# Order of the filter tables and a one-piece accumulating store in a depthwise layer on one core

## The chip, the cores and the metric

The kernel runs on one core of one Trainium2 chip. The metric is the time of one execution in microseconds (us) on the device. The kernel before was run three times: 5993.56, 6000.67 and 6012.33 us, median 6000.67. A further execution was profiled, and all rows below come from it.

## What is computed

The input x is 8 images of 32 channels of 512 x 512 float32. Two layers follow each other, each of the form x + f(normalised x), where the normalisation takes mean and variance over groups of two channels.

```python
x = x + _L0_conv_ref(_gn(x), L0_conv_weight, L0_conv_bias)
x = x + _L1_conv_ref(_gn(x), L1_conv_conv_w, L1_conv_conv_b)
```

Layer one is a quantised 3 x 3 convolution. Layer two first mixes the channels (a 1 x 1 convolution, `feat`), pools `feat` to a 5 x 5 filter for each image and channel, and applies each filter to its own channel (depthwise, 5 x 5, same size):

```python
feat = jnp.einsum('bihw,oi->bohw', x, conv_w) + conv_b[None, :, None, None]
filt = jnp.einsum('kh,bchw,lw->bckl', Ph, feat, Pw)
out = jax.lax.conv_general_dilated(inp, w, window_strides=(1, 1), padding=p,
        dimension_numbers=('NCHW', 'OIHW', 'NCHW'), feature_group_count=B * C)
```

The change touches only the second part of layer two, the depthwise product and its store.

## The kernel before

The kernel is one program of stages: `weights_and_masks`, `quantised_conv` (layer one, whose result x1 it writes to the output tensor in HBM), `statistics_of_x1`, `filters` (which writes the filters as tables to a scratch tensor in HBM), and `depthwise`, which this text is about.

`depthwise` walks through the 8 images, each cut into `BLOCKS` = 9 blocks of `ROWS_OUT` = 57 output rows (the last has 56), and each block into `STEPS` = 8 steps of four output channels. One step is a tile; an image has 72. Two kinds of product are made on TensorE in the same step. The pointwise product (lines 1053 to 1055) makes `feat` for the next block; the banded product (`banded`, line 1074, 36 matmuls a step) applies the filters to the block before, with a band matrix made from a table as the weights. Rows of the image lie in partitions, so that a tile of the result is 57 partitions of 4 channels x 512 columns.

The engines work in this order in one step. ScalarE splits x1 into a high part (`high`, line 966) and DVE into a low part (`low`, line 998); both copy the pointwise product out of PSUM (lines 979 and 1024); both evict half of the banded product into the slot `xr` of the tile (lines 988 and 1031). GpSimd then adds the slot to the output in HBM by an accumulating DMA (line 925), whose rows of 512 columns are single pieces of 2 KB.

There are `XR_SLOTS` = 4 slots. Before the eviction of tile m both engines wait in `wait_slot` until the store of tile m - 4 has landed (semaphore `stored[m % 4]`). The store is made as two transfers, of 48 rows (`SPLIT`) and of the other 9 (or 8 in the last block); each raises the semaphore by 16, so a slot counts 32 a tile. PSUM has two buffers for the banded product, which TensorE can refill only after both evictions.

SyncE issues all loads from one in-order queue. `load_x1` (line 851) loads a block of x1 for the block after the next, as four transfers. It waits until DVE has split the block whose buffer it takes, which is near step 6. `load_table` (lines 871 and 872) loads a quarter of the filter tables, eight channels, as four transfers of 48 or 13 rows and a bias transfer. There is one table buffer `tt` of 32 channels, so a quarter for the next image may be loaded only when the last block's steps have used it: quarter g is free after step 2g + 1. TensorE waits for quarter g (`t_loaded[g]`) at step 2g of the new image's first block. `group` on SyncE sets the order at the change of images (`j == N`): the quarters 0 and 1 stand at s = 5 and 7, x1 at s = 6, and quarters 2 and 3 follow at s = 7. Since every one of these places has its own wait, the number s only fixes the order: quarter 0, x1, quarter 1, 2, 3.

Of the kernel before, what the change touches and what calls it, by code (L numbers as in the profile page):

```python
# [5 lines left out]
ALU = mybir.AluOpType  # L6
# [33 lines left out]
STEPS = 8  # L40
XR_SLOTS = 4
# [3 lines left out]
SPLIT = 48  # L45
# [138 lines left out]
START = 1  # L184
# [572 lines left out]
def depthwise(nc, nb, k, rstd, table_d, bias_d, out):  # L757
# [6 lines left out]
    with ExitStack() as ctx:  # L764
# [17 lines left out]
        stored = [ctx.enter_context(nc.semaphore(f"c_stored{i}")) for i in range(XR_SLOTS)]  # L782
# [5 lines left out]
        band_done, even_out, odd_out = sem("c_band_done"), sem("c_even_out"), sem("c_odd_out")  # L788
        N = BLOCKS
        TILES = N * STEPS  # L790
# [3 lines left out]
        def valid(i):  # L794

            return (2 if i == 0 else 0), min(ROWS_IN, H + 2 - ROWS_OUT * i)

        def rows_out(i):
            return min(ROWS_OUT, H - ROWS_OUT * i)

        def xr_rows(m, lo, hi):

            base = PR * (m % XR_SLOTS % 2)
            return xr[base + lo:base + hi, m % XR_SLOTS // 2, :, :]
# [8 lines left out]
        def count(p, e, each, n):  # L813

            return p * (2 * each) + (e * each + n)

        def own(j):
            return j // N, j % N

        def another(p, e):  # L820

            return not (isinstance(p, int) and p == PAIRS - 1 and e == 1)

        def run(eng, group):

            group(0, 0, 0, True, False)
            if PAIRS > 1:
                with eng.Fori(0, PAIRS - 1) as p:
                    for e in range(2):
                        for j in range(1, N + 1):  # L830
                            group(p, e, j, True, True)
            for e in range(2):
                for j in range(1, N + 1):
                    group(PAIRS - 1, e, j, e == 0 or j < N, True)

        def x_slot(e, j):
            return (e * N + j) % 2

        def loads_of(p, e, j):

            return p * (N * Q * 16) + ((e * N + j) // 2 + 1) * (Q * 16)

        def load_x1(eng, p, e, j):

            if (e, j) not in ((0, 0), (0, 1)):
                eng.wait_ge(zl_done, count(p, e, STEPS * N, STEPS * (j - 1)) + START)
            de, i = own(j)
            lo, hi = valid(i)
            r0 = ROWS_OUT * i - 2
            for q in range(Q):  # L850
                eng.dma_start(xt[C * q:C * q + C, x_slot(e, j), lo:hi, :],  # L851
                              x1v[e + de::2][p, q, :, r0 + lo:r0 + hi, :]).then_inc(x1_loaded[x_slot(e, j)], 16)
# [3 lines left out]
        @block.sync  # L856
        def _(sp):

            def load_last_edge(p, e):

                sp.dma_start(tt[EDGE:EDGE + 1, :, :, :, :].rearrange("k o t w m -> k o (t w m)"),
                             bias_d[2:3, e::2, :, :][:, p, :, :]).then_inc(edge_loaded, 16)

            def load_table(p, e, g):
                for a in range(2):
                    for lo, hi in ((0, SPLIT), (SPLIT, ROWS_IN)):

                        src = table_d[e:nb:2][p, a, 8 * g * TROW + lo:8 * (g + 1) * TROW]
                        src = bass.AP(tensor=src.tensor, offset=src.offset, ap=[[1, hi - lo], [1, 8 * TROW]])
                        dst = tt[ROWS_IN * a + lo:ROWS_IN * a + hi, 8 * g:8 * g + 8, :, :, :]  # L870
                        sp.dma_start(dst.rearrange("k o t w m -> k (o t w m)"), src).then_inc(t_loaded[g], 16)  # L871
                sp.dma_start(tt[MAIN:EDGE + 1, 8 * g:8 * g + 8, :, :, :].rearrange("k o t w m -> k o (t w m)"),
                             bias_d[0:2, e::2, :, :][:, p, 8 * g:8 * g + 8, :]).then_inc(t_loaded[g], 16)

            def group(p, e, j, pointwise, banded):
                if not banded:
                    load_x1(sp, p, e, 0)
                    load_x1(sp, p, e, 1)
                    for g in range(4):
                        load_table(p, e, g)  # L880
                for s in range(STEPS):

                    if pointwise and j == N and s in (5, 7):
                        sp.wait_ge(band_done, count(p, e, TILES, TILES - STEPS + s - 3) + START)
                        load_table(p, e + 1, (s - 5) // 2)
                    if pointwise and j == N and s == 7:
                        for g in (2, 3):
                            sp.wait_ge(band_done, count(p, e, TILES, TILES - STEPS + 2 * g + 2) + START)
                            load_table(p, e + 1, g)
                    if s == 6 and pointwise and (j + 2 < N or another(p, e)):  # L890
                        load_x1(sp, p, e, j + 2)
                    if banded and j == 3 and s == 2:

                        sp.wait_ge(band_done, count(p, e, TILES, STEPS) + START)
                        load_last_edge(p, e)

            sem.start(sp)
            sp.wait_ge(cleared, 1 + START)
            run(sp, group)

        @block.gpsimd
        def _(pool):
            for m in range(XR_SLOTS):
                pool.dma_start(starter[0:1, m:m + 1], rstd[0:1, 0:1]).then_inc(stored[m], 16)  # L904

            for slot in range(2):
                pool.memset(feat[96:P, slot, 0, :, :], 1.0).then_inc(started, 1)  # L907
            pool.wait_ge(started, 6 + START)
            pool.memset(feat[:, :, :, :, 0:1].rearrange("p a b c d -> p (a b c) d"), 0.0)
            pool.memset(feat[:, :, :, :, FP - 1:FP].rearrange("p a b c d -> p (a b c) d"), 0.0).then_inc(cleared, 1)  # L910
            pool.wait_ge(cleared, 1 + START)

            def group(p, e, j, pointwise, banded):
                if not banded:
                    return
                if pointwise:

                    pool.wait_ge(x1_loaded[x_slot(e, j)], loads_of(p, e, j) + START)
                for s in range(STEPS):
                    m = STEPS * (j - 1) + s  # L920
                    n, r0 = rows_out(j - 1), ROWS_OUT * (j - 1)
                    pool.wait_ge(odd_out, count(p, e, TILES, m + 1) + START)
                    pool.wait_ge(even_out, count(p, e, TILES, m + 1) + START)
                    for lo, hi in ((0, SPLIT), (SPLIT, n)):
                        pool.dma_start(out[e::2][p, 4 * s:4 * s + 4, r0 + lo:r0 + hi, :].rearrange("c h w -> h c w"),  # L925
                                       xr_rows(m, lo, hi), accum_op=ALU.add).then_inc(stored[m % XR_SLOTS], 16)

            run(pool, group)
            for m in range(XR_SLOTS):
                pool.wait_ge(stored[m], nb * (TILES // XR_SLOTS) * 32 + 16)  # L930

        def positions(e, j, part):

# [18 lines left out]
                    tps[PR * h:PR * h + n, m % 2, :, :])  # L952

        def wait_slot(eng, p, e, m):
            eng.wait_ge(stored[m % XR_SLOTS], count(p, e, TILES // XR_SLOTS * 32, m // XR_SLOTS * 32) + 16)

        @block.scalar
        def _(act):
# [193 lines left out]
```

## Time and profile before

| | before |
|---|---|
| median of 3 runs | 6000.67 us (5993.56 to 6012.33) |
| profiled execution, its own time | 5992.25 us |
| its span | 5990.5 us |
| TensorE busy | 4829.2 us, 81% of the span |
| VectorE (DVE) busy | 4582.7 us, 76% |
| ScalarE (ACT) busy | 3994.4 us, 67% |
| GpSimd (POOL) busy | 1384.6 us, 23% |
| mean granted TensorE clock | 0.909 of full speed |
| layer two (first to last banded product) | 2722.8 to 5978.4 us of the span |

A row of a profile says what an engine did or what it waited for. PE is TensorE, PEld its weight load, DVE is VectorE, ACT is ScalarE, POOL is GpSimd, SP is SyncE; SPq is SyncE's queue, on which DMAs are issued. L1074 is line 1074 of the kernel. All times are us unless marked. An arrow `<-` between an engine's line and something else means "was released by". "DMA share" is the mean busy share of the core's 16 DMA engines; it can be above 1 since packets overlap. "Landing" is the time from a DMA's issue to its completion.

### The profile page before, as it was taken

What the parts mean: (1) busy time and instruction counts of PE and PEld (TensorE: products, weight loads), DVE (VectorE), ACT (ScalarE), POOL (GpSimd) and SP (SyncE); (2) the same over time, 40 slices, a digit from 0 to 9 for tenths busy, and PEclk for the clock granted to TensorE, in tenths of its full rate; (3) what the DMA queues carried; (4) which work ended last, traced back from release to release, by engine and by line L of the source; (5) the groups of instructions that cost most, each with busy time, mean ns of one, the idle gap of its engine ahead of it and who ended that gap; (6) DMA issues with size and microseconds to landing.
All of it is one profiled execution on the core that took longest, in us unless ns stands there. A gap on an engine that the chain in (4) does not pass through costs nothing.

```text
span 5990.5 us, 113135 instructions
## 1 busy us (share of the span) xinstructions
PE 4829.2 (81%) x43798; PEld 3263.0 (54%) x43798; DVE 4582.7 (76%) x5363; ACT 3994.4 (67%) x2509; POOL 1384.6 (23%) x1698
## 2 busy tenths in 40 slices
PE   0767767666667767918998989989989899899899
PEld 0111111111111111207988979979979789799798
DVE  6787878777787878747887868868868778688686
ACT  1646565655555556807877868868868778688686
POOL 0111111111111111112332323323323333233233
PEclk9888878888888888958999999989999999999999
DMA  9999999999999998949999999999999999999997
GB/s 263 278 276 301 301 287 302 281 302 273 319 261 322 271 312 242 287 96 184 180 196 179 180 193 183 181 190 182 188 192 180 197 179 180 188 189 178 188 190 125
DMA packets 1065164, 1347.06 MB, mean 225 GB/s; under 512 B 78330, under 2 KB 636666, under 8 KB 1060602
## 3 DMA queue, kind: packets, MB, share of 16 engines
q1 hardware_dynamic: 749506, 657.45, 49.3%
q0 software_dynamic: 240000, 537.11, 39.9%
q10 hardware_dynamic: 75072, 144.72, 8.3%
q8 instruction: 364, 5.96, 0.4%
q14 instruction: 222, 1.82, 0.1%
HBM read 800.10 MB, written 538.84 MB: 224 GB/s over the span
## 4 chain that ended last, share of the span: by engine, by line
PE 48%; SPq 4%; DMA 2%; DVE 0%; issue 0%; POOL 0%; ACT 0%; DVEq 0%; POOLq 0%; ACTq 0%
PE c_tps L1074 36%; PE c_cps L1053 4%; PE c_cps L1054 4%; PE c_cps L1055 4%; SPq L851 3%; DMA c_tt<-bias_scratch 2%; SPq L871 1%; DMA c_x<-out_dram 1%; DVE c_z L998 0%; POOL c_feat L907 0%; ACT c_z L966 0%; DVE c_xr L1031 0%; POOL c_starter L904 0%; POOL out_dram L925 0%; ACT c_feat L979 0%
## 5 line engine op out<-in xcount | busy, mean ns | idle before, releaser
L1074 PE MATMUL c_tps<-c_feat,c_tt 123*128 123x256 f16 (+1 forms) x20736 | 2385.6, 273 | 169.3 <-DMA c_tt<-bias_scratch 167.5
L1074 PEld LDWEIGHTS c_tps<-c_feat,c_tt 123*128 123x128 f16 (+1 forms) x20736 | 1998.8, 98 | 428.1 <-DMA c_tt<-bias_scratch 134.8
L925 POOL DMA_DIRECT2D out_dram<-c_xr x1152 | 1056.5, 1054 | 2266.3 <-DVE c_xr L1031 2105.9
L440 PE MATMUL b_ps<-b_xq,w0main 128*128 128x512 bf16 x3072 | 950.1, 415 | 679.5 <-ACT b_q L398 540.3
L966 ACT ACTIVATE c_z<-c_x,c_rs 128x976 f16<-128x976 f32 x576 | 1150.2, 1997 | 116.1 <-DMA c_x<-out_dram 116.1
L1031 DVE TENSOR_SCALAR c_xr<-c_tps 57x1024 f32<-57x1024 f32 (+1 forms) x576 | 701.5, 1218 | 686.1 <-PE c_tps L1074 686.1
L998 DVE SCALAR_TENSOR_TENSOR c_z<-c_x,c_rs,c_z 128x976 f16<-128x976 f32 x576 | 1105.9, 1920 | 69.6 <-ACT c_z L966 47.0
L398 ACT ACTIVATE b_q<-b_ps,q_bias 128x1024 int8<-128x1024 f32 x512 | 547.6, 1115 | 787.3 <-DVE b_x L518 728.8
L988 ACT ACTIVATE c_xr<-c_tps 57x1024 f32<-57x1024 f32 (+1 forms) x576 | 639.2, 1110 | 629.0 <-PE c_tps L1074 628.9
L440 PEld LDWEIGHTS b_ps<-b_xq,w0main 128*128 128x128 bf16 x3072 | 225.6, 101 | 1351.3 <-issue 1094.1
L453 PE MATMUL b_ps<-b_xq,w0edge 64*32 64x512 bf16 x3048 | 918.5, 411 | 0.0
L450 PE MATMUL b_ps<-b_xq,w0edge 64*32 64x512 bf16 x3048 | 915.7, 411 | 0.0
L1053 PE MATMUL c_cps<-w_high,c_z 128*128 128x128 f16 x4608 | 813.4, 221 | 124.4 <-DVE c_z L998 112.9
L979 ACT ACTIVATE c_feat<-c_cps 122x1024 f16<-122x1024 f32 x576 | 822.7, 1428 | 121.3 <-PE c_cps L1055 119.3
L573 POOL DMA_DIRECT2D out_dram<-b_x x512 | 298.9, 584 | 2254.8 <-DVE b_cols L533 2061.7
L1024 DVE TENSOR_TENSOR c_feat<-c_cps,c_feat 122x1024 f16<-122x1024 f32 x576 | 810.2, 1407 | 7.9 <-ACT c_feat L979 7.7
L1055 PE MATMUL c_cps<-w_high,c_z 128*128 128x128 f16 x4608 | 811.7, 220 | 0.0
L1054 PE MATMUL c_cps<-w_low,c_z 128*128 128x128 f16 x4608 | 811.2, 220 | 0.0
L477 DVE BATCH_NORM_STATS2 b_stats_x<-b_stream 128x6 f32<-128x512 f32 x672 | 414.4, 680 | 438.8 <-DMA b_stream<-in_x_dram 401.9
L529 DVE BATCH_NORM_STATS2 b_stats<-b_x 128x6 f32<-128x408 f32 (+5 forms) x1520 | 645.3, 500 | 3.9
L518 DVE SCALAR_TENSOR_TENSOR b_x<-b_q,b_x 128x2048 f32<-128x2048 int8 x256 | 574.8, 2281 | 65.4 <-ACT b_q L398 65.4
L383 ACT ACTIVATE b_x<-b_x,b_shift,b_scale 128x4096 int8<-128x4096 f32 x128 | 487.0, 3805 | 139.8 <-issue 101.8
(131 smaller groups left out, 2732.2 us busy)
## 6 DMA issues: line engine op xcount, KB each, us to landing
out_dram<-b_x POOLq DMA_DIRECT2D x512, 512.0 KB, 11.2
out_dram<-c_xr POOLq DMA_DIRECT2D x576, 384.0 KB, 7.9
c_x<-out_dram SPq DMA_DIRECT2D x224, 976.0 KB, 21.9
b_stream<-in_x_dram SPq DMA_DIRECT2D x672, 256.0 KB, 12.7
b_x<-in_x_dram ACTq DMA_DIRECT2D x276, 512.0 KB, 13.3
b_x<-in_x_dram SPq DMA_DIRECT2D x276, 512.0 KB, 12.4
c_tt<-table_scratch SPq DMA_DIRECT2D x64, 576.0 KB
out_dram<-c_xr POOLq DMA_DIRECT2D x512, 72.0 KB, 9.2
```

What stands on the lines that cost most here:

```text
L440: return pe.matmul(ps[:, g % 3, j, :], k.w0main[:, d, :, :].rearrange("p r o -> p (r o)"), xq[:, n % XQ_SLOTS, 2 * i + j, d:d + W], start= ...
L450: pe.matmul(ps[0:C, g % 3, j, :], k.w0edge[P // 2:P, d, :], xq[P // 2:P, (m - 1) // JB % XQ_SLOTS, (m - 1) % JB, d:d + W], start=False, st ...
L453: pe.matmul(ps[P - C:P, g % 3, j, :], k.w0edge[0:P // 2, d, :], xq[0:P // 2, (m + 1) // JB % XQ_SLOTS, (m + 1) % JB, d:d + W], start=False ...
L925: pool.dma_start(out[e::2][p, 4 * s:4 * s + 4, r0 + lo:r0 + hi, :].rearrange("c h w -> h c w"), xr_rows(m, lo, hi), accum_op=ALU.add).then ...
L966: act.activation(split_part(0, part), positions(e, j, part), ACT.Identity, scale=scale_of(e, j)).then_inc(zh_done, 1)
L979: act.activation(dst, cps[0:MAIN, s % 2, :, :].rearrange("p j (q o) -> p o q j", q=Q), ACT.Identity).then_inc(fh_done, 1)
L998: dve.scalar_tensor_tensor(split_part(1, part), positions(e, j, part), scale_of(e, j), split_part(0, part), ALU.mult, ALU.subtract).then_i ...
L1024: dve.tensor_tensor(lo, cps[0:MAIN, s % 2, :, :].rearrange("p j (q o) -> p o q j", q=Q), hi, ALU.subtract).then_inc(fl_done, 1)
L1053: pe.matmul(dst, zh, wh, start=True, stop=False)
L1054: pe.matmul(dst, zh, wl, start=False, stop=False)
L1055: last = pe.matmul(dst, zl, wh, start=False, stop=True)
L1074: last = pe.matmul(tps[:, s % 2, o % 4, :], tt[0:rows, o, tp, 2 * d:2 * d + 2, :].rearrange("k w m -> k (w m)"), feat[0:rows, (e * N + i) ...
```

## The change

On SyncE, at the change of images, quarter 1 of the table is issued ahead of the load of x1: the order becomes quarter 0, quarter 1, x1, quarter 2, quarter 3. Each quarter's wait is for the same step as before. On GpSimd the two accumulating transfers of a tile become one of all its rows (57, or 56 in the last block), and the counts of the slot semaphores are halved accordingly.

```diff
                 for s in range(STEPS):

-                    if pointwise and j == N and s in (5, 7):
-                        sp.wait_ge(band_done, count(p, e, TILES, TILES - STEPS + s - 3) + START)
-                        load_table(p, e + 1, (s - 5) // 2)
-                    if pointwise and j == N and s == 7:
+                    if pointwise and j == N and s in (2, 4):
+                        sp.wait_ge(band_done, count(p, e, TILES, TILES - STEPS + s) + START)
+                        load_table(p, e + 1, s // 2 - 1)
+                    if s == 6 and pointwise and (j + 2 < N or another(p, e)):
+                        load_x1(sp, p, e, j + 2)
+                    if pointwise and j == N and s == STEPS - 1:
                         for g in (2, 3):
                             sp.wait_ge(band_done, count(p, e, TILES, TILES - STEPS + 2 * g + 2) + START)
                             load_table(p, e + 1, g)
-                    if s == 6 and pointwise and (j + 2 < N or another(p, e)):
-                        load_x1(sp, p, e, j + 2)
...
-                    for lo, hi in ((0, SPLIT), (SPLIT, n)):
-                        pool.dma_start(out[e::2][p, 4 * s:4 * s + 4, r0 + lo:r0 + hi, :].rearrange("c h w -> h c w"),
-                                       xr_rows(m, lo, hi), accum_op=ALU.add).then_inc(stored[m % XR_SLOTS], 16)
+                    pool.dma_start(out[e::2][p, 4 * s:4 * s + 4, r0:r0 + n, :].rearrange("c h w -> h c w"),
+                                   xr_rows(m, 0, n), accum_op=ALU.add).then_inc(stored[m % XR_SLOTS], 16)
...
-                pool.wait_ge(stored[m], nb * (TILES // XR_SLOTS) * 32 + 16)
+                pool.wait_ge(stored[m], nb * (TILES // XR_SLOTS) * 16 + 16)
...
-            eng.wait_ge(stored[m % XR_SLOTS], count(p, e, TILES // XR_SLOTS * 32, m // XR_SLOTS * 32) + 16)
+            eng.wait_ge(stored[m % XR_SLOTS], count(p, e, TILES // XR_SLOTS * 16, m // XR_SLOTS * 16) + 16)
```

## Rows read from the trace of the kernel before

**Rows 1.** The page's chain that ended last: shares of the span by line.

```profile
PE c_tps L1074 36%; PE c_cps L1053 4%; PE c_cps L1054 4%; PE c_cps L1055 4%; SPq L851 3%; DMA c_tt<-bias_scratch 2%; SPq L871 1%; DMA c_x<-out_dram 1%; DVE c_z L998 0%; POOL c_feat L907 0%; ACT c_z L966 0%; DVE c_xr L1031 0%; POOL c_starter
```

**Rows 2.** The chain in time at the first image change: start, us, what.

```profile
3096.88 3.95 PE c_tps L1074 x36
...
3148.34 13.50 DMA c_tt<-bias_scratch
3161.89 5.72 PE c_tps L1074 x36
...
3168.95 3.95 PE c_tps L1074 x36
...
3174.24 3.95 PE c_tps L1074 x36
```

**Rows 3.** TensorE's waits (total us, times, longest): layer two, then 3100 to 3200 us.

```profile
PE c_tps L1074 <- DMA c_tt<-bias_scratch: 167.5, 7, 29.1
...
PE c_tps L1074 <- DMA c_tt<-bias_scratch: 27.7, 1, 27.7
```

**Rows 4.** SyncE's timeline at the first image change: start, us, line, transfers.

```profile
3095.44 8.66 SPq L871 DMA_DIRECT2D c_tt<-table_scratch  x4
3104.29 0.24 SPq L872 DMA_DIRECT2D c_tt<-bias_scratch  x1
3114.84 23.97 SPq L851 DMA_DIRECT2D c_x<-out_dram  x4
3139.09 9.07 SPq L871 DMA_DIRECT2D c_tt<-table_scratch  x4
3148.34 0.24 SPq L872 DMA_DIRECT2D c_tt<-bias_scratch  x1
```

**Rows 5.** Stretches: length, busy PE, PEld, DVE, ACT, POOL; PEclk, DMA share, GB/s.

```profile
3115.00:3135.00 20.00, 19.07 (x220) 17.21 (x217) 16.33 (x12) 16.20 (x12) 5.91 (x8) 1.00 1.13 211
3135.00:3162.00 27.00, 0.11 (x1) 0.12 (x2) 2.39 (x2) 2.37 (x2) 1.74 (x2) 0.55 1.10 209
```

**Rows 6.** DMA issues, whole span: count, KB each, median us to landing.

```profile
out_dram<-c_xr POOLq DMA_DIRECT2D x576, 384.0 KB, 7.9
c_x<-out_dram SPq DMA_DIRECT2D x224, 976.0 KB, 21.9
...
c_tt<-table_scratch SPq DMA_DIRECT2D x64, 576.0 KB
out_dram<-c_xr POOLq DMA_DIRECT2D x512, 72.0 KB, 9.2
...
c_tt<-table_scratch SPq DMA_DIRECT2D x64, 156.0 KB
...
c_tt<-bias_scratch SPq DMA_DIRECT2D x32, 24.0 KB
...
c_starter<-rstd POOLq DMA_DIRECT2D x4, 0.0 KB, 2.5
```

**Rows 7.** GpSimd's timeline after the stall: start, us, [idle before].

```profile
3169.68 1.87 POOL L925 DMA_DIRECT2D out_dram<-c_xr  x2 [32.94 <-DVE c_xr L1031]
3174.97 1.83 POOL L925 DMA_DIRECT2D out_dram<-c_xr  x2 [3.42 <-DVE c_xr L1031]
```

**Rows 8.** DMA traffic 5933.2 to 5939.2 us, one tile's store and no loads.

```profile
DMA packets 289, 0.48 MB, mean 81 GB/s; under 512 B 60, under 2 KB 60, under 8 KB 288
...
q0 software_dynamic: 288, 0.47, 57.2%
...
out_dram<-c_xr POOLq DMA_DIRECT2D x2, 384.0 KB, 4.8
out_dram<-c_xr POOLq DMA_DIRECT2D x2, 72.0 KB, 5.0
```

**Rows 9.** The store queue 3134 to 3142 us, beside x1's loads: packets, MB, share.

```profile
q0 software_dynamic: 490, 0.79, 55.2%
```

**Rows 10.** GB/s of all DMA in 40 slices, 3200 to 3242 us.

```profile
GB/s 241 218 214 232 279 197 181 209 198 262 244 225 220 272 178 178 196 195 200 189 216 139 74 77 82 174 149 39 78 183 145 132 163 151 193 215 212 252 217 209
```

## Prediction

> **What bounds the kernel now.** I read the chain that ended last first: it runs mostly on TensorE, in the banded product of line 1074 [rows 1]. In layer two a step is 5.29 us, the distance of two banded starts [rows 2], and there are 8 images x 9 blocks x 8 steps = 576 of them, 3,047 us. The list of waits comes second: line 1074 waits for only one thing, the table loads, 7 times for 167.5 us together and 29.1 us at most [rows 3]. Seven is the number of image changes. The third view, SyncE's timeline around the first change, shows why: table 0 is issued at 3095.44, then four loads of x1 from 3114.84 to 3138.8, and only then table 1, whose last piece is issued at 3148.34 and lands 13.50 us later, at 3161.84 [rows 2, 4]. In that instant line 1074 starts again [rows 2]; without the wait its start would have been 27.7 us earlier, at 3134.2 [rows 3]. Last, the table of stretches says what table 1 waited for: while TensorE stood still the DMA share was 1.10 and 209 GB/s moved, and just before it 1.13 [rows 5]. The sixteen DMA engines had no air at all; the table was late because they were full, not only because it was issued late.
>
> **Part one, the order of the tables.** SyncE's order at an image change was table 0, x1, table 1, 2, 3; it becomes table 0, 1, x1, 2, 3. Each table is still four pieces and a bias, (576 + 156) x 2 + 24 = 1,488 KB [rows 6]; nothing is added. Table 1's channels are free after the last block's step 3, at 3096.88 + 3.95 = 3100.83 [rows 2], so it can follow table 0, whose issue ends at 3104.53 [rows 4]. Its data would pass before x1's and be there by 3134.2: step 2 of the new image no longer waits. What is late next is table 2, which step 4 needs, two steps later at 3134.2 + 2 x 5.29 = 3144.7, and which still stands behind x1 (3.9 MB). The DMA engines must move the same bytes as before up to table 1's landing, plus table 2 (1.52 MB) and the stores of the two tiles that TensorE now makes meanwhile (2 x 0.47 MB): 2.46 MB at 209 GB/s are 11.8 us. Table 2 so lands at 3161.84 + 11.8 = 3173.6, and step 4 started at 3174.24 before [rows 2]. Gain: 0.6 us a change, 4 us in seven. The stall moves from step 2 to step 4 and is 3173.6 - 3144.7 = 28.9 us there in place of 27.7; the two steps that stood behind it, 12.4 us with their slow start [rows 2], stand ahead of it and take 10.6. The moved issue has x1 behind it: four loads come up to 1.52 MB / 209 GB/s = 7.3 us later, about 3168, and they are read first some steps after step 4, so nobody waits. The bounds: at best the queue had room, table 2 lands when table 1 did, and two steps are saved each time, 7 x 10.6 = 74 us; at worst table 1 itself is some 2 us late, 15 us. I take 4 us, since the share of over 1.0 leaves no room [rows 5].
>
> **Part two, one store of 57 rows.** It removes one issue on GpSimd per tile. GpSimd spends 1.8 us of each step on both and idles 3.4 us before the next [rows 7]; nobody waits for it but the landing, so this is worth nothing. What counts is when the transfer lands: tile m+4 may be evicted only when tile m's store is in. A store is issued 3169.68 - (3161.89 + 5.72) = 2.1 us after its last product [rows 2, 7], and the slot is wanted four steps later, so the budget is 4 x 5.29 - 2.1 = 19.1 us. Now the two pieces take 7.9 and 9.2 us [rows 6], 4.8 and 5.0 us where no load runs beside them [rows 8].
>
> How 57 rows are shared among 16 engines no row shows directly. What the last-image window shows: one tile puts 288 packets on the queue, 60 of them tiny [rows 8]. 57 rows x 4 channels are 228 pieces of 2 KB, which leaves 60 = 2 x 16 semaphore updates + 28, and 28 is 7 x 4: seven engines got fillers in place of the 9-row piece's four entries. So whole rows go to engines, one each on nine. 48 is three each on sixteen. Every transfer of this queue has equal shares (32, 48, 9, 8 rows). 57 = 3 x 19 has equal shares only on three engines (or one): 19 rows, 76 pieces each. Uneven shares would be four rows on most of fifteen engines, 16 pieces. I take three engines, as the nearest rows all have equal shares.
>
> The price of a piece: a transfer of nothing lands in 2.5 us [rows 6], so alone it is (4.8 - 2.5) / 12 = 0.19 us; with x1's loads in flight the queue moved 0.79 MB, 386 pieces, in 8 us on 16 engines, 0.33 us a piece [rows 9]. 76 pieces then land in 2.5 + 76 x 0.19 = 17 us alone, and in 2.5 + 76 x 0.33 = 28 us beside loads. The first is under the budget, the second over it. Loads fill about 29 us of a block of 42.3: in the 42 us window the first 21 slices and the last 7 of 40 are the fast ones [rows 10]. A transfer of over 20 us seldom lies wholly inside, so I take the middle, 23 us: a slot turns round in 23 + 2.1 us, a step in 25.1 / 4 = 6.3. 29 us hold 4.6 such steps, the other 3.4 take 18 us, the block 47 in place of 42.3: 4.7 us x 64 blocks = 300 us. (The ninth block of each image has 56 rows, equal on fourteen engines, 16 pieces: no cost.) Bounds: 17 us throughout costs nothing; 28 us throughout makes every step (28 + 2.1) / 4 = 7.5 us, x 512 steps = +1,140 us. Less than nothing only if fewer semaphore updates relieve the engines: 16 of 288 packets, tiny ones, under 5 us in all.
>
> The Trainium skill, page DMA: Bandwidth & Descriptors, section on why a DMA increments its semaphore by 16, says that a copy runs on the largest number of engines up to 16 that divides its slowest dimension; by it 57 rows have 3 and 56 have 14, as I take them. The same page's rules for kernel authors speak the other way for the merge, since two transfers to disjoint partitions share the engines anyway; by them this part would cost nothing.
>
> **Sum.** The profiled execution is 5992.25 us (span 5990.5), 8 us under the median of the three runs shown. 5992 - 4 + 300 = 6288, say 6290.
>
> **The rivals.** (a) Uneven shares: 57 rows on fifteen engines. 16 pieces land in 2.5 + 16 x 0.33 = 7.8 us, far inside 19.1; the time is 5988, no change. For it: the fillers show that the hardware can pad an engine that has nothing to do [rows 8]. Against it: no transfer here is uneven. The same page of the Trainium skill names an exception in which some copies from GpSimd use all 16 engines with rounded-up shares; no run here shows it, and it would be this case. (b) Three engines, but GpSimd's queue gets a larger part of each engine than 0.33 us a piece says: 76 pieces land within 19 us (0.22 us each), and again nothing changes, about 5990. For it: a single queue's 0.19. (c) The other side: the table's stall was one of order. Place: the image change; price: the two steps, 74 us, so 5918, provided that (a) or (b) holds too. It decides where table 2 lands before 3171, that is, where x1 isn't delayed by table 1; the engines would need 2.5 us of air between 3104 and 3134. Against it the share of 1.13 [rows 5]. Half of its price would already be seen. (d) The load's rate on three shared engines falls below what I take and the transfers run at 28 us or more: 5992 + 1,140 = 7,130.
>
> **How the numbers follow.** Three engines with a price (forecast, with (d) at its upper end): 0.68. (a) 0.15 and (b) 0.07: no change. (c) 0.10. A measurement of this kernel can tell about 0.3% (18 us) from none. So faster 0.10, same 0.22, slower 0.68. The forecast case's own range is 6080 to 6800. The whole range must take in (a) and (b) and leaves out (c)'s full price and (d)'s extreme: 5960 to 6800.
>
> **What would show it.** Right: GpSimd's store, now 456 KB, lands in about 17 us in the last block but one and over 20 us beside loads, 8 us at the 56-row blocks; DVE's and ScalarE's evictions of lines 1031 and 988 wait for the DMA of c_xr, and line 1074 for them; steps of over 6 us in the first two thirds of a block. Line 1074's waits for tables stay near 24 us a change, two steps later than before, with the bias of table 2 last. Wrong: landings of 8 to 10 us and steps of 5.29 (then (a)); or the waits for tables down to about 14 us each (then (c)).

## The result, and the profile after

The changed kernel takes 6335.86 us (6317.32 to 6360.93, 4 runs) against 6000.73 us of the kernel before, a ratio of 1.0558 with a 95% interval of 1.0523 to 1.0593. The forecast was 6290 us, the range 5960 to 6800. The profiled execution has a span of 6348.3 us, 357.8 us more than before.

The page of the changed kernel, in the parts that answer to [rows 1, 6]: the DMA queue of the stores, the chain that ended last, the two lines of TensorE and GpSimd, and the stores with their landing. All line numbers of `depthwise` behind the store are one lower than before.

```profile
q0 software_dynamic: 722304, 541.01, 41.8%
...
DMA out_dram<-c_xr 23%; SPq L851 9%; PE c_tps L1073 8%; DMA c_x<-out_dram 6%; DVE c_z L997 2%; DMA c_tt<-bias_scratch 2%; SPq L871 1%; DVE c_xr L1030 1%; PE c_cps L1052 1%; PE c_cps L1054 1%; PE c_cps L1053 1%; ACT c_xr L987 0%; ACT c_z L965 0%; POOL c_feat L907 0%; ACT c_feat L978 0%
...
L1073 PE MATMUL c_tps<-c_feat,c_tt 123*128 123x256 f16 (+1 forms) x20736 | 2415.1, 275 | 244.5 <-DMA c_tt<-bias_scratch 230.0
...
L924 POOL DMA_DIRECT2D out_dram<-c_xr x576 | 1098.0, 1906 | 2579.3 <-DVE c_xr L1030 2102.7
...
out_dram<-c_xr POOLq DMA_DIRECT2D x512, 456.0 KB, 19.8
c_x<-out_dram SPq DMA_DIRECT2D x224, 976.0 KB, 26.4
```

The chain that ended last no longer runs on TensorE's line (8% in place of 36%) but on the landing of the stores, 23%, and on x1's loads, 9% for their issue and 6% for their landing. A store lands in 19.8 us in place of 7.9 and 9.2 [rows 6]. And one issue on GpSimd costs 1906 ns, 1098.0 us in all, where the 1,152 issues of before took 1056.5 us of busy time together; the merge has saved GpSimd nothing.

The waits in layer two of the changed kernel (total us, times, longest):

```profile
DVE c_xr L1030 <- DMA out_dram<-c_xr: 497.5, 201, 11.3
ACT c_xr L987 <- DMA out_dram<-c_xr: 470.8, 191, 11.2
...
PE c_tps L1073 <- DMA c_tt<-bias_scratch: 230.0, 8, 40.2
PE c_cps L1052 <- DVE c_z L997: 227.4, 124, 21.4
...
ACT c_z L965 <- DMA c_x<-out_dram: 171.6, 38, 25.3
```

The same list of the kernel before has these two rows for the last two:

```profile
PE c_cps L1053 <- DVE c_z L998: 24.1, 7, 15.4
...
ACT c_z L966 <- DMA c_x<-out_dram: 19.3, 1, 19.3
```

The first two rows did not exist before: 201 of 576 tiles waited for their slot. TensorE feels it through the low parts that DVE makes late, 227.4 us where it was 24.1. The third row answers to [rows 3]: tables cost 62.5 us more. The last one was 19.3 us before: now x1 itself is late 38 times. TensorE's idle time before its two leading lines grew by 244.5 - 169.3 = 75 and by 325.9 - 124.4 = 202 us (whole span), its busy time by 4914.4 - 4829.2 = 85 us for the same products. The longer busy time goes with a lower granted clock: 0.898 of full speed over the span where it was 0.909. In a long stretch of layer two, first before and then after (columns as in [rows 5]):

```profile
4000.00:5400.00 1400.00, 1327.73 (x14953) 1210.14 (x14951) 1105.03 (x757) 1092.04 (x748) 456.72 (x498) 0.97 1.02 186
...
4000.00:5400.00 1400.00, 1215.72 (x13302) 1090.81 (x13300) 978.38 (x677) 970.99 (x666) 421.76 (x221) 0.94 0.99 168
```

The granted clock fell from 0.97 to 0.94, a mean over stretches at full speed and slower ones: in [rows 5] it is 1.00 while TensorE works and 0.55 in the stall. The DMA engines are as busy as before, 0.99 against 1.02, and yet move 168 GB/s where they moved 186.

How a stretch within an image looks, GpSimd's timeline of the changed kernel:

```profile
3341.81 2.01 POOL L924 DMA_DIRECT2D out_dram<-c_xr  x1 [2.50 <-DVE c_xr L1030]
3346.86 2.01 POOL L924 DMA_DIRECT2D out_dram<-c_xr  x1 [3.04 <-DVE c_xr L1030]
3351.29 2.01 POOL L924 DMA_DIRECT2D out_dram<-c_xr  x1 [2.42 <-DVE c_xr L1030]
3358.45 2.02 POOL L924 DMA_DIRECT2D out_dram<-c_xr  x1 [5.15 <-DVE c_xr L1030]
3367.43 2.02 POOL L924 DMA_DIRECT2D out_dram<-c_xr  x1 [6.95 <-DVE c_xr L1030]
```

The distances are 5.1, 4.4, 7.2 and 9.0 us: no even step of 6.3 but short steps and long ones, a slot that comes late and the catching up behind it. Over the second to eighth blocks of all images the mean distance is 5.8 us, where it was 5.3.

**Where 57 rows go.** The count of packets settles it. Before, both kinds of tile put 288 packets on the store queue (228 + 28 + 32, and in the last block 224 + 32 + 32). If 57 rows go to three engines, 76 pieces each, and the other 13 engines get as many fillers, a tile has 228 + 13 x 76 + 16 = 1,232 packets; with 56 rows on 14 engines it has 224 + 2 x 16 + 16 = 272. The growth is then 944 x 512 - 16 x 64 = 482,304. The page of before has

```profile
q0 software_dynamic: 240000, 537.11, 39.9%
```

and the page after 722304: the difference is 482,304, exactly. Uneven shares on fifteen engines would have lowered the count. The trace also has the size and the time of each packet: in the changed kernel 507,904 packets of this queue have 8 bytes and took 10.6 ns each, together 337 us per engine; before there were 16,384 of them, 11 us per engine. The 196,608 large pieces took 192 ns each before and 188 after. So the fillers added 326 us of packet time to each of the sixteen engines.

### The profile page after: what moved, and what is told of

Its sections match the earlier page's. It is cut to its first block, busy times and chain, and to the rows that moved or that the text cites. A ratio compares the mean times of both kernels' runs of the same rounds, so it can differ in the third digit from the quotient of the medians.

```text
span 6348.3 us, 111695 instructions
## 1 busy us (share of the span) xinstructions
PE 4914.4 (77%) x43798; PEld 3293.0 (52%) x43798; DVE 4570.9 (72%) x5363; ACT 3994.5 (63%) x2509; POOL 1427.7 (22%) x1122
## 3 DMA queue, kind: packets, MB, share of 16 engines
q0 software_dynamic: 722304, 541.01, 41.8%
## 4 chain that ended last, share of the span: by engine, by line
DMA 30%; SPq 11%; PE 10%; DVE 3%; issue 2%; ACT 1%; POOL 0%; POOLq 0%; ACTq 0%; DVEq 0%
DMA out_dram<-c_xr 23%; SPq L851 9%; PE c_tps L1073 8%; DMA c_x<-out_dram 6%; DVE c_z L997 2%; DMA c_tt<-bias_scratch 2%; SPq L871 1%; DVE c_xr L1030 1%; PE c_cps L1052 1%; PE c_cps L1054 1%; PE c_cps L1053 1%; ACT c_xr L987 0%; ACT c_z L965 0%; POOL c_feat L907 0%; ACT c_feat L978 0%
## 5 line engine op out<-in xcount | busy, mean ns | idle before, releaser
L1073 PE MATMUL c_tps<-c_feat,c_tt 123*128 123x256 f16 (+1 forms) x20736 | 2415.1, 275 | 244.5 <-DMA c_tt<-bias_scratch 230.0
L924 POOL DMA_DIRECT2D out_dram<-c_xr x576 | 1098.0, 1906 | 2579.3 <-DVE c_xr L1030 2102.7
L1030 DVE TENSOR_SCALAR c_xr<-c_tps 57x1024 f32<-57x1024 f32 (+1 forms) x576 | 699.9, 1215 | 931.3 <-DMA out_dram<-c_xr 497.5
L1052 PE MATMUL c_cps<-w_high,c_z 128*128 128x128 f16 x4608 | 835.7, 224 | 325.9 <-DVE c_z L997 313.4
L1054 PE MATMUL c_cps<-w_high,c_z 128*128 128x128 f16 x4608 | 835.3, 224 | 0.0
L1053 PE MATMUL c_cps<-w_low,c_z 128*128 128x128 f16 x4608 | 834.0, 224 | 0.0
L1052 PEld LDWEIGHTS c_cps<-w_high,c_z 128*128 128x128 f16 x4608 | 460.9, 100 | 369.4 <-DVE c_z L997 349.0
## 6 DMA issues: line engine op xcount, KB each, us to landing
out_dram<-c_xr POOLq DMA_DIRECT2D x512, 456.0 KB, 19.8
b_stream<-in_x_dram SPq DMA_DIRECT2D x672, 256.0 KB, 12.5
```

The lines of the kernel that those rows point to most:

```text
L924: pool.dma_start(out[e::2][p, 4 * s:4 * s + 4, r0:r0 + n, :].rearrange("c h w -> h c w"), xr_rows(m, 0, n), accum_op=ALU.add).then_inc(sto ...
L1052: pe.matmul(dst, zh, wh, start=True, stop=False)
L1053: pe.matmul(dst, zh, wl, start=False, stop=False)
L1054: last = pe.matmul(dst, zl, wh, start=False, stop=True)
L1073: last = pe.matmul(tps[:, s % 2, o % 4, :], tt[0:rows, o, tp, 2 * d:2 * d + 2, :].rearrange("k w m -> k (w m)"), feat[0:rows, (e * N + i) ...
```

## The experiments

Each kernel ran on the same chip as the kernel before, in rounds with it; a difference is one of medians.

**The order of the tables alone.** Only the hunk on SyncE is applied.

```diff
-                    if pointwise and j == N and s in (5, 7):
+                    if pointwise and j == N and s in (2, 4):
...
```

> The order of the tables alone, the store still in two pieces of 48 and 9 rows. Theory A (the order is worth nothing since the DMA engines are full at the image change): 4 us faster than before, within 15 us; TensorE's waits for tables stay at about 170 us in all, two steps later. Rival C (the order is a cause of the slowdown, because x1 comes later): 50 us slower or more. Rival D (the stall was one of order): 60 to 74 us faster, table waits down to about 95 us.

Measured: 5997.63 against 5993.57 us, ratio 1.0009 (0.9995 to 1.0023). No change, as theory A has it. The waits of TensorE in this kernel, and SyncE's timeline at its first image change:

```profile
PE c_tps L1074 <- DMA c_tt<-bias_scratch: 159.4, 7, 25.9
```

```profile
3111.95 1.81 SPq L871 DMA_DIRECT2D c_tt<-table_scratch  x4
3113.99 0.24 SPq L872 DMA_DIRECT2D c_tt<-bias_scratch  x1
3122.36 33.84 SPq L851 DMA_DIRECT2D c_x<-out_dram  x4
3156.46 8.43 SPq L871 DMA_DIRECT2D c_tt<-table_scratch  x4
3165.07 0.24 SPq L872 DMA_DIRECT2D c_tt<-bias_scratch  x1
```

Quarter 1 is issued ahead of x1, the four issues of x1 take 33.84 us where they took 23.97 [rows 4], and quarter 2, which is needed two steps later, comes as late for its need as quarter 1 had come: TensorE waits 25.9 us for it at this change, where it waited 27.7. The stall has moved and hardly shrunk.

**The single store alone.** Only the hunks on GpSimd and the semaphore counts are applied.

> The single store of 57 rows alone, tables in the old order. Theory A (57 rows go to three engines): all of the slowdown, 320 to 340 us slower than before; 988 tiny filler packets a tile, landing near 20 us. Rival C: clearly less than the change as a whole, under 280 us.

Measured: 6327.10 against 5993.57 us, 334 us more, ratio 1.0551 (1.0516 to 1.0586). This is the whole of the slowdown.

**Two pieces, cut at 54 rows.**

```diff
-                    for lo, hi in ((0, SPLIT), (SPLIT, n)):
+                    for lo, hi in ((0, 54), (54, n)):
```

> Two pieces as before, cut at 54 rows instead of 48. Theory A (equal shares: 54 rows on nine engines, 6 rows or 24 pieces each; 3 rows on three): the large piece lands in about 2.5 + 24 x 0.33 = 10.4 us, inside the budget of 19.1, so no change, within 20 us of before. Rival E (uneven shares, rounded up, and the slowdown comes from something else in the single transfer): 54 rows land like 48, in 8 us, no change either; the count of fillers tells them apart (A: 7 x 24 + 13 x 4 = 220 a tile, E: 8 + 52 = 60 or so).

Measured: 6054.94 us, 61 us more, ratio 1.0093 (1.0068 to 1.0119). The shares are theory A's to the packet: 192 more a tile x 576 = 110,592, and the queue has 350,592 in place of 240,000. But the time was not expected by either theory. The waits of this kernel:

```profile
PE c_tps L1074 <- DMA c_tt<-bias_scratch: 211.6, 7, 34.0
...
ACT c_z L966 <- DMA c_x<-out_dram: 83.3, 43, 24.6
...
DVE c_xr L1031 <- DMA out_dram<-c_xr: 1.4, 1, 1.4
```

No slot is waited for (1.4 us). What costs is that tables and x1 come later: TensorE waits 44.1 us more for tables, ScalarE 64.0 us more for x1. There is a second way in which a store on fewer engines costs, and it does not go by the slots.

**Two pieces, cut at 51 rows.** The same edit with 51.

> Two pieces as before, cut at 51 rows = 3 x 17. Theory A: three engines with 17 rows, 68 pieces each; landing about 0.9 of the single store's 19.8 us, near 18 us; as slow as the whole change or a little less, 200 to 320 us slower than before, although it is cut in two and larger by only three rows than 48. Rival E (the cost belongs to making one transfer of it): no change. In the last block 51 rows of 56 are also slow here, which adds 1/8 more tiles.

Measured: 6643.88 us, 650 us more, ratio 1.1083 (1.1059 to 1.1107). So it is not the one transfer in place of two: a cut that is larger by three rows than 48 is slower than no cut at all. The packets are again exact: 51 rows on three engines and 6 on six give 1,184 a tile, 896 x 576 = 516,096 more, measured 756,096 - 240,000. The waits of DVE for slots are 752.9 us. That it is twice as slow as the single store was not expected.

A good part of the surprise lies in the last block of each image. There 51 of 56 rows still go to three engines, where the single store has all 56 on fourteen. The landing of the second piece, which is the last of its tile, in the other blocks and in the last ones, and a stretch of layer two (columns as in [rows 5]):

```profile
out_dram<-c_xr POOLq DMA_DIRECT2D x512, 48.0 KB, 19.9
...
out_dram<-c_xr POOLq DMA_DIRECT2D x64, 40.0 KB, 28.4
```

```profile
4000.00:5400.00 1400.00, 1118.03 (x12081) 997.08 (x12082) 890.46 (x614) 882.79 (x604) 563.21 (x404) 0.91 0.87 154
```

By the issues in the trace, the eight last blocks take 496 us together, against 371 us in the kernel with the single store alone: 125 us of the 317 us between the two. The first blocks, which come behind them, take 670 against 614 us; the rest is spread over the other blocks. The DMA share is 0.87, so on average the engines have air here, which they have not with the single store. Why the last block's stores take 28.4 us is not shown.

**The single store with six slots.** The space comes from `z`, the tiles of high and low parts, which go from four slots to two; the clearing of `z` is cut to fit.

```diff
-XR_SLOTS = 4
+XR_SLOTS = 6
...
-Z_SLOTS = 4
+Z_SLOTS = 2
...
```

> The single store of 57 rows with six slots instead of four (tables in the old order; the space comes from z, two slots instead of four). Theory A (a landing of about 20 us and up to 28 beside loads against a budget of 19.1): with six slots the budget is 6 x 5.29 - 2.1 = 29.6 us, so the waits for the stores' landing (497.5 us of DVE in the changed kernel) fall below 50 us and most of the slowdown goes: 20 to 100 us slower than the kernel before. What stays is what cutting at 54 rows cost without any slot wait, 50 to 60 us, through later loads. Rival F (the DMA engines as a whole have lost throughput): still over 250 us slower.

**The same six slots with the split store,** as a control.

> Control of the six slots: the split store of before with six slots and z in two. Both theories: no change, within 20 us of before, since nothing waits for a slot there. If it is slower, that is the price of the smaller z, and is taken off the other run.

Measured: the control takes 5989.26 against 5998.05 us, ratio 0.9990 (0.9975 to 1.0004), so the smaller z costs nothing. The single store takes 6255.16 us, 257 us more, ratio 1.0422 (1.0405 to 1.0439). The waits of layer two in it:

```profile
ACT c_z L965 <- DMA c_x<-out_dram: 304.6, 46, 31.1
...
PE c_tps L1073 <- DMA c_tt<-bias_scratch: 221.6, 7, 35.3
```

The waits for slots have left the list, as theory A said, but only 77 us of the 334 went with them. They were replaced: ScalarE now waits 304.6 us for x1 where it waited 182.2 us with the single store and four slots. So with enough slots the store's shape still holds up the loads that share the engines. Of the two theories F is nearer in size, and A right on the waits alone.

**Little of x1 to load.** After the first two blocks only 8 of the 61 rows are loaded; the split with the stale rows that remain is made as before, so the work on the engines is the same and its result isn't the reference's.

```diff
             r0 = ROWS_OUT * i - 2
+            if (e, j) not in ((0, 0), (0, 1)):
+                hi = lo + 8
             for q in range(Q):
```

> The kernel before with x1's loads cut to 8 of 61 rows after the first two blocks (the product is then made of stale rows). Every theory: the stall at the image change shrinks, since the engines have air: waits for tables from 167.5 us to under 40, 120 to 160 us faster than before.

> The single store with the same cut loads. Theory A: alone a 57-row store lands in about 17 us, inside the budget of 19.1, so nothing waits for slots and the time equals that of the split store with cut loads, within 25 us. Rival G (the single store is too slow by itself): still over 150 us slower than the split store with cut loads.

Measured: 5823.42 us with the split store (175 us less than before, more than expected; no wait for tables is left) and 5888.25 us with the single one. The single store costs 65 us here, where it costs 334 beside full loads. Its landing in the kernel with cut loads, and DVE's wait:

```profile
out_dram<-c_xr POOLq DMA_DIRECT2D x512, 456.0 KB, 17.9
```

```profile
DVE c_xr L1032 <- DMA out_dram<-c_xr: 283.8, 149, 9.3
```

17.9 us is the estimate of 17, and it is so near to the budget of 19.1 that 149 tiles still wait a little. Theory A said within 25 us and G over 150; it lies between, nearer to A. The other 269 us need the loads. The mean DMA share from 4000 to 5400 us is 0.72 and 0.71 in these two kernels, so here the engines have air for the fillers.

**Two pieces of 38 and 19 rows.** The same edit as above with 38.

> Two pieces, 38 = 2 x 19 and 19 rows: two engines and one, so the same 76 pieces on the same three engines a tile as the single store, and a landing near 20 us. Only the fillers differ: 14 x 76 + 15 x 76 = 2,204 a tile instead of 988. Theory H (new: the fillers themselves cost engine time, about 9 ns each spread over 16 engines, in a layer that keeps the DMA engines full): 1,216 x 512 x 9.1 ns / 16 = 350 us more than the single store, about 680 us slower than before. Rival I (the cost is the three engines that carry it all, which hold up the loads): the same as the single store, 310 to 350 us slower than before.

Measured: 7310.69 against 5991.96 us, 1,319 us more, ratio 1.2208 (1.2183 to 1.2233). Both theories are far off. The packets are once more as the shares say: 2,464 a tile of 57 rows, 1,376 a tile of 56 (38 on two engines, 18 on nine), 1,183,744 more, measured 1,423,744 - 240,000. What is new stands in this kernel's waits:

```profile
POOL out_dram L925 <- issue: 1774.0, 466, 18.8
ACT c_xr L988 <- DMA out_dram<-c_xr: 1682.6, 475, 14.8
DVE c_xr L1031 <- DMA out_dram<-c_xr: 1675.3, 473, 14.9
```

GpSimd itself stands still for 1,774 us before its issues for a reason that no other engine's work shows, 466 times, where this was 124.9 us in the kernel before. The trace tells what it stands still for. In the second to eighth blocks each of the 448 tiles has its first issue 0.2 to 0.45 us after the store of the tile three before has landed, with the stores of two tiles still under way; in the changed kernel only 6 tiles have that distance, and mostly three tiles are under way at an issue. So the four slots of the program work as three. A tile takes 22.7 us from its first issue to its last landing (median outside the last blocks), and (22.7 + 0.3) / 3 = 7.7 us is nearly the mean distance of two tiles in these blocks, 7.6 us, where it was 5.3: they take 1,044 us more than before, most of the 1,319.

A queue that holds a limited number of entries, fillers among them, would look like this: each engine gets 152 entries a tile here, 76 with the single store and 16 before. In the last blocks, where a tile has 84 entries an engine, three tiles are again under way at 50 of 64 issues. The dependence on entries is a reading of these counts and not a separate test. The DMA share of this kernel falls too:

```profile
4000.00:5400.00 1400.00, 1044.31 (x10588) 913.97 (x10589) 776.13 (x535) 769.02 (x529) 693.75 (x353) 0.89 0.87 133
```

So neither H, by which the engines' time is the price, nor I is what bounds this kernel.

**Fillers without large pieces.** The kernel before, with one more small transfer a tile (and a wait for the one four tiles earlier).

```diff
+                    pool.dma_start(few_to[0:1, m % 4, :, 0:1], few_from[0:1, :, 0:1],
+                                   allow_slow_non_contiguous=True).then_inc(few[m % 4], 16)
```

> The kernel before plus, per tile, one tiny transfer on GpSimd's queue inside SBUF: 66 separate elements of one partition. It goes to one engine and should bring 15 x 66 = 990 fillers a tile, as many as the single store, with no engine loaded by large pieces; the store stays split in 48 and 9 rows. Theory H: 990 x 576 x 9.1 ns / 16 = 320 us slower than before. Rival I: under 60 us slower, the price of one more small transfer.

Measured: 6001.88 against 5991.96 us, 10 us more, ratio 1.0015 (1.0004 to 1.0026). It does not decide anything between H and I, since the fillers weren't made: the queue has 258,560 packets, 18,560 more, which is 32 a transfer (and 128 of four starters). The queue carried 16 packets of 10 to 20 bytes and 16 semaphore updates for each transfer, not 66 and 990. It shows that one more small transfer a tile costs about 10 us.

**The ring of engines shifted.** The single store and a transfer of six partitions, one element each.

```diff
+                    pool.dma_start(tiny_d[e::2][p, m:m + 1, 0:6].rearrange("a r -> r a"),
+                                   rstd[0:6, 0:1]).then_inc(tiny[m % 2], 16)
```

> The single store plus one tiny transfer of six partitions (one element each) to a scratch tensor per tile. Theory J (a transfer of k engines takes the next k in a ring of sixteen, so after 57 rows the ring moves by 3 a tile, and with six more by 9, when every second tile shares an engine with the one before the last): as slow as the 51 and 6 cut, 500 to 700 us slower than before, landings with a median over 22 us. Rival K (which engines come next plays no part; the 51 and 6 cut was slower for another reason): as the single store, 310 to 370 us slower.

Measured: 6350.53 us, 359 us more, ratio 1.0588 (1.0570 to 1.0606), with a median landing of 19.7 us. That is in rival K's range, 25 us more than the single store's 334 us, with one more transfer a tile. No count here shows that the ring of engines was shifted; if it was, it does not cost what J said. J was my explanation of why 51 and 6 is slower than 57, and it falls as far as it was tested.

**All tables ahead of x1.** The kernel before, with its split store.

```diff
                 for s in range(STEPS):

-                    if pointwise and j == N and s in (5, 7):
-                        sp.wait_ge(band_done, count(p, e, TILES, TILES - STEPS + s - 3) + START)
-                        load_table(p, e + 1, (s - 5) // 2)
-                    if pointwise and j == N and s == 7:
-                        for g in (2, 3):
+                    if pointwise and j == N and s == 6:
+                        for g in range(4):
                             sp.wait_ge(band_done, count(p, e, TILES, TILES - STEPS + 2 * g + 2) + START)
                             load_table(p, e + 1, g)
```

> The kernel before with all four quarters of the table issued ahead of x1 at the image change. If the stall is the engines' work alone, the order that serves first what is wanted first (steps 2, 4 and 6 for the tables, about step 8 for x1) leaves no air behind the stall: waits for tables nearly gone, a wait of ScalarE for x1 of about 20 us a change in their place, 0 to 50 us faster than before in all. If x1's later load pushes the next ones too: up to 50 us slower.

Measured: 5924.71 (5921.94 to 5931.50) against 5991.96 us, ratio 0.9889 (0.9872 to 0.9905), 67 us faster than before and so faster than both kernels. Its waits of ScalarE and TensorE in layer two:

```profile
ACT c_z L963 <- DMA c_x<-out_dram: 117.3, 8, 21.3
PE c_cps L1050 <- DVE c_z L995: 100.8, 18, 17.4
```

No wait for tables is left in its list; in its place ScalarE waits for x1, 117.3 us, longest 21.3. TensorE's idle before both lines falls from 169.3 + 35.7 us in layer two to 100.8 + 12.5 + 17.1 + 4.3 = 134.7 us. The gain comes from the air that the kernel before has behind its stall, which its table of stretches shows (columns as in [rows 5]):

```profile
3162.00:3180.00 18.00, 18.00 (x186) 15.82 (x186) 10.57 (x8) 10.31 (x8) 3.70 (x4) 0.91 0.78 146
3180.00:3190.00 10.00, 10.00 (x117) 9.15 (x116) 8.26 (x6) 8.31 (x6) 3.67 (x4) 1.00 0.65 91
```

The DMA engines were full up to the stall's end and partly idle after it. In the kernel with all tables first the share is 1.04 from 3162 to 3180 us and 1.15 from 3180 to 3200 us: the air is gone. Serving x1 last, which is wanted last, lets TensorE work through more steps before anything must be complete.

## Why the prediction was right, and where its steps were not

**The order of the tables: right.** It was priced at 4 us from the bytes that must pass before quarter 2; measured alone it makes 1.0009 (0.9995 to 1.0023). The stall moved to quarter 2, as forecast. It was to grow from 27.7 to 28.9 us at the first change and is 25.9. Rival (c) is refuted in this form; the price that it named is nearly there, though, for another order (67 of 74 us).

**Three engines for 57 rows: right, shown by counts.** The queue's packets agree exactly with equal shares of whole rows for all five cuts that ran (57, 54, 51, 48 and 38 rows). The Trainium skill's rule (DMA: Bandwidth & Descriptors, the section on why a DMA increments its semaphore by 16) holds in all of them, and its exception with rounded-up shares, rival (a), occurs in none. Its rules for kernel authors advise one 128-partition transfer in place of two over disjoint halves. Carried over to 48 and 9 rows, as the prediction did for the merge, that advice fails: one transfer of 57 rows costs 334 us.

**The landing: right alone, a bit low in the middle.** 17 us was estimated without loads; 17.9 is the median with cut loads, and 16.9 that of the last three 57-row stores of the changed kernel. Beside loads the median is 19.8, not 23 nor 28, with single ones up to 34.0 us (the median runs over stretches with and without loads). The 56-row blocks were to land in 8 us; their median is 16.2 and only in the last stretch, 6300 to 6348 us, 6.0. That was the first failed step: I took 16 pieces of their own, with neither the stores ahead of them in the queue nor the tables beside them. The kernel with cut loads separates the two. Its last blocks, the last image's left out, have median landings of 19.2, 15.1 and 12.5 us for the first three tiles, behind stores of 57 rows; about 5.6 us for the next three; and 22 and 24 us for the last two, beside the tables.

```profile
out_dram<-c_xr POOLq DMA_DIRECT2D x64, 448.0 KB, 16.2
```

```profile
out_dram<-c_xr POOLq DMA_DIRECT2D x8, 448.0 KB, 6.0
```

**The sum of 300 us: right in size (334 and 335), by luck.** I put all of it on the slots: a budget of 19.1 us, a landing of 23 and steps of 6.3. The waits for slots are there, 497.5 us on DVE. But with six slots, when they are gone, 257 us remain, and only 77 went with them. Two terms were wrong, and they made up for each other.

The first is the landing of 23 us. With the measured 19.8 my own sum gives a turn of 19.8 + 2.1 us, a step of 5.5, and, worked out as before, about 1 us a block: an estimate of 63 us in place of 300. That is near to the 77 us that six slots gave back and to the 65 us with cut loads. A piece costs (19.8 - 2.5) / 76 = 0.23 us beside loads and not 0.33, which is nearly what rival (b) named; its forecast of no change fails all the same, through the other term.

The second is what the store does to the loads, which I charged nothing. "Fewer semaphore updates" of tiny packets was all that I counted on the DMA engines' side, under 5 us. In fact the fillers grew the queue by 482,304 packets. The queue in the kernels with 54 and 3 rows, with six slots, with 51 and 6 rows and with 38 and 19 rows:

```profile
q0 software_dynamic: 350592, 537.99, 40.3%
...
q0 software_dynamic: 722368, 541.01, 42.6%
...
q0 software_dynamic: 756096, 541.24, 40.1%
...
q0 software_dynamic: 1423744, 546.58, 42.5%
```

The queue's packets took 39.9% of 5990.5 = 2,390 us before and 41.8% of 6348.3 = 2,654 us after, per engine: 264 us more in a layer whose engines were full, against 335 measured. (The fillers took 326 us more, the large pieces and the semaphore updates about 60 us less.) With the cut at 54 rows it is 40.3% of 6049.6 us, 48 us more, against 61; with six slots 42.6% of 6237.2, 267 more, against 257. In the other kernels the two don't agree: 272 against 650 (51 and 6), 714 against 1,319 (38 and 19), where the DMA share fell to 0.87 and something else holds the tiles up, and nothing against 65 with cut loads, where the engines had air. So where the engines stay full, the time grows about as the packets' time does. That speaks for the fillers, since the large pieces took no longer than before. It isn't a test: whether it is the fillers' time or the unevenness, three engines that hold up every load that spreads over sixteen, isn't decided, because the kernel that was to make fillers alone did not make them. Both effects come from the same shares.

The sum also left out the granted clock, with which TensorE's busy time grew by 85 us. And the waits for stores don't show on line 1074, as I had said, where TensorE waits 4.8 us for DVE's evictions, but at the pointwise product, 227.4 us behind DVE's low parts.

**Waits for tables** were to stay near 24 us a change and rose to 230.0 / 7 = 33 us (the eighth of the waits is one of 2 us). The kernel with the cut at 54 rows has 30 us a change without any wait for slots, and the single store alone 33; so it is the second way again.

**Open.** How the single store's 257 us divide between fillers and unevenness. Why the last block's stores land in 28.4 us with 51 and 6 rows: GpSimd's own stalls are small there (223.0 us of idle before an issue), and the one cause that I tested, which engines follow each other, made no difference as I tested it. Whether the stop of GpSimd with 38 and 19 rows goes by the number of entries. The single store with a fourth kind of relief, fewer fillers on the same three engines, wasn't tried.

## What to carry to other kernels

Cut a transfer over partitions so that its large piece divides evenly among all sixteen engines and only a small one doesn't (48 and 9, not 57, 51 or 54), and count the queue's packets in the profile: with equal shares the count is a number that you can work out beforehand, and a jump in it tells at once how a transfer was spread. One transfer fewer is worth nothing if the issuing engine has idle time, and its issue may cost what the two had cost. A total that comes out right is no proof of its terms: the six slots and the cut loads took this one apart.

When loads queue up behind full DMA engines, moving one of them forward only moves the stall. Issue them in the order in which their data are wanted and compare the sum of bytes up to each need with the rate: here the whole order (tables, then x1) gave 1.1%, one swap gave nothing.

## What was not expected of the hardware

The accumulating stores on GpSimd's queue put the same number of entries on all sixteen engines, with packets of 8 bytes on those that carry no rows; the counts of five cuts agree with it exactly. Here that made 482,304 more packets of 10.6 ns each for the same rows, and 541.01 MB moved where it was 537.11. GpSimd's issue takes longer the more entries each engine gets: a pair of issues takes 1.84 us with 12 and 4 entries, 2.79 with 68 and 4 and 4.02 with 76 and 76; one issue with 76 takes 2.01. With 152 entries an engine a tile, GpSimd did not issue a tile's stores before the store of the tile three before had landed.
